# Row sums of the diagonal key tiles over GpSimd pairs, and W2 butterflies in blocks of three and five, in a two-layer adaLN kernel

## The reference, cut to what matters

```python
qkv = x @ W_qkv + b_qkv                      # 16 heads of 32
scores = jnp.einsum('bhqd,bhkd->bhqk', q, k) / np.sqrt(HEAD_DIM)
scores = jnp.where(causal, scores, NEG)      # causal, 2048 x 2048
probs = jax.nn.softmax(scores, axis=-1)
ctx = jnp.einsum('bhqk,bhkd->bhqd', probs, v)
...
hidden = fwht(silu(x @ W1.T) * (x @ W3.T))   # Walsh-Hadamard over 2048
out = hidden @ W2.T
```

## Time and profile before

| | us | share of the span |
|---|---|---|
| median of three executions | 2040.35 | |
| profiled execution | 2039.48 | |
| its span | 2037.5 | 100% |
| PE busy | 1942.6 | 95% |
| PE weight loads busy | 1392.5 | 68% |
| DVE busy | 1066.4 | 52% |
| ACT busy | 636.8 | 31% |
| POOL busy | 470.9 | 23% |

### The profile page before, as it was taken

One profiled execution on the slowest core, in us unless ns is written; L12 is line 12 of the kernel. 1 busy time (PEld: TensorE's weight loads), 2 busy tenths in 40 slices (PEclk: granted clock), 3 DMA queues, 4 the chain that ended last, 5 costly groups with the idle time before them and its releaser, 6 DMA issues. The chain is left out here.

```text
span 2037.5 us, 25525 instructions
## 1 busy us (share of the span) xinstructions
PE 1942.6 (95%) x10068; PEld 1392.5 (68%) x10068; DVE 1066.4 (52%) x1836; ACT 636.8 (31%) x1153; POOL 470.9 (23%) x409
## 2 busy tenths in 40 slices
PE   6999999999999998899999999997999889999998
PEld 4677545555555544688888888885787668888886
DVE  4456877676666633853434343435442674434334
ACT  3231345555555564332111211113221241111111
POOL 0122666667645166300000000002000510000000
PEclk9999999999999998999999999999999899999999
DMA  9654422421421103110000000002000011000002
GB/s 316 220 162 134 95 53 44 95 53 44 94 43 33 33 2 135 57 42 32 26 6 32 31 32 1 1 1 86 11 6 11 21 42 41 32 22 21 6 1 83
DMA packets 61718, 111.84 MB, mean 55 GB/s; under 512 B 6000, under 2 KB 21248, under 8 KB 61568
## 3 DMA queue, kind: packets, MB, share of 16 engines
q1 hardware_dynamic: 54144, 85.05, 14.5%
q0 software_dynamic: 7456, 25.18, 4.2%
HBM read 84.77 MB, written 25.44 MB: 54 GB/s over the span
## 5 line engine op out<-in xcount | busy, mean ns | idle before, releaser
L452 DVE TENSOR_REDUCE part_max<-banks 128x1 f32<-128x512 f32 (+2 forms) x640 | 357.2, 614 | 153.4 <-PE banks L424 93.5
L923 ACT ACTIVATE probs<-banks 128x512 f32<-128x512 f32 (+3 forms) x640 | 310.6, 539 | 279.7 <-PE banks L850 141.0
L424 PE MATMUL banks<-kst,qst 96*128 96x512 f32 (+2 forms) x640 | 261.1, 416 | 12.8 <-DVE part_max L452 9.1
L846 PE MATMUL banks<-qst,kst 98*128 98x512 f32 (+2 forms) x640 | 250.7, 412 | 0.2 <-ACT probs L923 0.2
L1448 DVE TENSOR_TENSOR tokens_a<-banks,tokens_a 128x512 f32<-128x512 f32 x224 | 151.5, 688 | 69.8 <-PE banks L216 69.0
L1473 DVE TENSOR_TENSOR tokens_b<-banks,tokens_b 128x512 f32<-128x512 f32 x64 | 44.2, 691 | 258.3 <-ACT tokens_b L1392 258.2
L214 PE MATMUL banks<-f_d_hi,f_hid_hi 128*128 128x512 f32 x432 | 170.0, 393 | 6.7 <-issue 3.6
L214 PE MATMUL banks<-h_hi,f_w_first 128*128 128x512 f32 x448 | 174.6, 390 | 0.0
L216 PE MATMUL banks<-h_hi,f_w_first 128*128 128x512 f32 x448 | 174.4, 389 | 0.0
L215 PE MATMUL banks<-h_lo,f_w_first 128*128 128x512 f32 x448 | 174.3, 389 | 0.0
L216 PE MATMUL banks<-f_d_hi,f_hid_lo 128*128 128x512 f32 x432 | 168.3, 389 | 0.0
(11 more groups left out here) (192 smaller groups left out, 3269.6 us busy)
## 6 DMA issues: line engine op xcount, KB each, us to landing
tokens_a<-in_L_wmod SPq DMA_DIRECT2D x12, 1024.0 KB, 7.0
qst<-q_hi SPq DMA_DIRECT2D x32, 256.0 KB, 6.1
kst<-k_hi SPq DMA_DIRECT2D x32, 256.0 KB, 8.3
x<-in_L_attn_x SPq DMA_DIRECT2D x4, 1024.0 KB, 13.2
q_hi<-qk_out_hi POOLq DMA_DIRECT2D x16, 256.0 KB, 3.1
q_lo<-qk_out_lo POOLq DMA_DIRECT2D x16, 256.0 KB, 3.2
k_hi<-qk_out_hi POOLq DMA_DIRECT2D x16, 256.0 KB, 4.2
k_lo<-qk_out_lo POOLq DMA_DIRECT2D x16, 256.0 KB, 4.3
```

What stands on the lines that cost most here:

```text
L424: mm = nc.tensor.matmul(dst[:, 0:wide], qst[n % QS][0:BIASROW, h, P * t:P * t + P], kst[(NB * g + c) % KS][0:BIASROW, h, 0:wide], start=Tr ...
L452: nc.vector.tensor_reduce(part_max[:, n % 2, ht, c:c + 1], max_bank(slot)[:, 0:wide], AX_X, ALU.max).then_inc(max_read, 1)
L846: mm = nc.tensor.matmul(dst[:, c0:512], kst[ck % KS][0:BIASROW + 2, h, at:at + P], qst[n % QS][0:BIASROW + 2, h, c0:512], start=True, stop ...
L923: nc.scalar.activation(probs[:, q % PS, h, c0:512], score_bank(sh)[:, c0:512], ACT.Exp, scale=SCALE).then_inc(exp_done, 1)
```

## The change

Diagonal steps become pairs too. In the first diagonal step POOL adds the two tiles over the 384 queries that both see, in the second over the 128 that both see. PE sums the pair with one set of that width, and the 128 queries that only the step's first tile sees with another set of width 128 (`narrow_sums`). Only the first step of blocks 0, 4, 8 and 12 stays as it was. The sum of a diagonal pair stands right behind the step's own context matmuls. The diagonal's pair index counts on with the others (76 pairs instead of 48), so that ACT, DVE and SP wait for them: ACT before it overwrites the tiles, DVE before it transposes bank 7, SP before it loads the projection's weights.

The butterflies of a slice are cut: three behind the first diagonal step's pair, five behind the second's. The slice's store and the next slice's load follow the eighth, and loads now alternate between two buffers.

```diff
-                return off_before(n) + i
+            pair_index = {}
+            for s, (n, i) in enumerate(steps):
+                if off_diagonal(s) or n % NB or i:
+                    pair_index[s] = len(pair_index)
+            def pair_column(s):
+                n, i = steps[s]
+                return P * max(2 * i + 1 - TB * (n % NB), 0)
...
-                sp.wait_ge(pairs_used, off_before(NQ))
+                sp.wait_ge(pairs_used, len(pair_index))
...
+                    if step % 8 == 7:
+                        pool.wait_ge(fw_step, step + 1)
+                        pool.dma_start(w2m[:, :, FW * c:FW * c + FW], fw[c % 2]).then_inc(fw_stored, 16)
+                        if c + 1 < SLICES:
+                            load_columns(c + 1)
...
-                        nc.gpsimd.tensor_tensor(pairs[o % 2][:, h, :], probs[:, 2 * s % PS, h, :],
-                                                probs[:, (2 * s + 1) % PS, h, :], ALU.add).then_inc(pair_ready, 1)
+                        nc.gpsimd.tensor_tensor(pairs[o % 2][:, h, c0:512], probs[:, 2 * s % PS, h, c0:512],
+                                                probs[:, (2 * s + 1) % PS, h, c0:512], ALU.add).then_inc(pair_ready, 1)
...
-                    if off_diagonal(s):
+                    if s in pair_index:
                         add_pair(s)
-                    elif i == 2 * (n % NB) and n in mixed_at:
-                        butterflies(mixed_at[n])
+                    if not off_diagonal(s) and n in mixed_at:
+                        for step in range(0, 3) if i == 2 * (n % NB) else range(3, 8):
+                            butterfly(8 * mixed_at[n] + step)
...
-                        if not diagonal:
+                        if paired:
+                            if diagonal and half == 0:
+                                mm = narrow_sums(s)
                             mm.then_inc(probs_read, 1)
-                    if not diagonal:
+                    if paired:
+                        if diagonal:
+                            sum_pair(s)
                         return
...
+                def narrow_sums(s):
+                    n, i = steps[s]
+                    at = first_column(n, 2 * i)
+                    for h in range(4):
+                        mm = nc.tensor.matmul(bank[7][HD * h:HD * h + HD, at:at + P], ones[:],
+                                              probs[:, 2 * s % PS, h, at:at + P], start=False, stop=False)
+                    return mm
...
-                            if q >= PS and off_diagonal(s - 2):
-                                act.wait_ge(pair_ready, 4 * off_index(s - 2) + h + 1)
+                            if s - 2 in pair_index:
+                                act.wait_ge(pair_ready, 4 * pair_index[s - 2] + h + 1)
...
                         dve.wait_ge(probs_read, quads_before(n + 1))
+                        dve.wait_ge(pairs_used, pair_index[steps.index((n, 2 * j + 1))] + 1)
```

More of the change, by code:

```diff
@@ L777, in attend_gpsimd @@
                 w2m = w2_mixed.rearrange("(c p) d -> p c d", p=P)
[L779 to L795, removed]
+                SLICES = D // FW
@@ new lines, in load_columns, with butterfly @@
+                def load_columns(c):
+                    pool.dma_start(fw[c % 2], w2[:, :, FW * c:FW * c + FW]).then_inc(fw_loaded, 16)
+                def butterfly(step):
+                    c, r, odd = step // 8, step % 8 // 2, step % 2
+                    if step % 8 == 0:
+                        pool.wait_ge(fw_loaded, 16 * (c + 1))
+                        if c:
+                            pool.wait_ge(fw_stored, 16 * c)
+                    elif odd == 0:
+                        pool.wait_ge(fw_step, step)
+                    half = 1 << r
+                    src = fw[(c + r) % 2].rearrange("p (a b h) d -> p a b (h d)", b=2, h=half)
+                    dst = fw[(c + r + 1) % 2].rearrange("p (a b h) d -> p a b (h d)", b=2, h=half)
+                    nc.gpsimd.tensor_tensor(dst[:, :, odd, :], src[:, :, 0, :], src[:, :, 1, :],
+                                            ALU.subtract if odd else ALU.add).then_inc(fw_step, 1)
+                    if step % 8 == 7:
[3 more added lines that the diff above has]
+                            load_columns(c + 1)
@@ L797, in add_pair @@
                 def add_pair(s):
-                    o = off_index(s)
+                    o, c0 = pair_index[s], pair_column(s)
                     if o >= 2:
@@ L862, in sum_pair @@
                     n, i = steps[s]
-                    o = off_index(s)
+                    o, c0 = pair_index[s], pair_column(s)
                     pe.wait_ge(pair_ready, 4 * (o + 1))
                     for h in range(4):
-                        mm = nc.tensor.matmul(bank[7][HD * h:HD * h + HD, :], ones[:], pairs[o % 2][:, h, :],
-                                              start=(i == 0), stop=False)
+                        mm = nc.tensor.matmul(bank[7][HD * h:HD * h + HD, c0:512], ones[:], pairs[o % 2][:, h, c0:512],
+                                              start=(i == 0), stop=(i == 2 * (n % NB) + 1))
                     mm.then_inc(pairs_used, 1)
@@ L879, in context @@
                         pe.wait_ge(ones_ready, 3)
+                    paired = s in pair_index
                     for half in range(2):
@@ L897, in context @@
                             mm = nc.tensor.matmul(bank[7][HD * h:HD * h + HD, c0:512], ones[:],
-                                                  probs[:, q % PS, h, c0:512], start=(kt == 0),
-                                                  stop=(last and half == 1))
+                                                  probs[:, q % PS, h, c0:512], start=(kt == 0), stop=False)
                         mm.then_inc(probs_read, 1)
+                def narrow_sums(s):
[5 more added lines that the diff above has]
+                    return mm
                 for s, (n, i) in enumerate(steps):
```

9 lines of the change are left out of this document (2 added, 7 removed).

## The result

| | before | changed |
|---|---|---|
| median of six executions, us | 2040.59 | 2031.45 |
| lowest and highest | 2036.48 to 2042.89 | 2026.07 to 2033.62 |
| ratio, 95% interval | | 0.9951 (0.9940 to 0.9962) |
| span of the profiled execution | 2037.5 | 2030.1 |

The change takes 9.1 us by the medians, 7.8 to 12.2 by the interval. The forecast was 2033.0, a gain of 7.4 against the median shown then; the sum behind it was 6.5, and that lies outside the interval.

What follows compares the result with a forecast made beforehand. PE's own work was taken as the bound (busy 95% of the span). 10.2 us of PE less waits of 0.25, 1.2, 1.2, 0.7 and 0.3 gave 6.5, from 2039.48 to 2033.0 us; range 2029 to 2039.

Steps and rivals of the forecast that it cites:

- PE's columns: Diagonal row sums on PE: 0.61 us gained in each of 12 first steps, 0.18 in 16 second, 10.2 in all.
- The subtraction that gave 0.25: Second diagonal step: 0.68 us for sets of 256 and 128, less 0.43 for 256 columns, leaves 0.25 for 128.
- the gain passes DVE: Block 9: DVE idles 3.47 and 0.41 us, longer than the 0.61 and 0.18 gained, so it starts earlier by as much.
- POOL's adds: New diagonal adds on POOL: 1.01 us at width 384, 0.45 at 128, from a line through widths 512 and 256.
- The waits: PE waiting for POOL in blocks 14, 15 and into 7, plus the last load: 3.65 us off the gain.
- Block 7: Start of block 7: its first pair comes late behind five butterflies and two DMA issues on POOL; PE waits 0.7 us.
- Second diagonals: Second diagonal steps of blocks 14 and 15: PE waits 0.6 us each for POOL's pair, 1.2 for two.
- The last load: Projection's weights and gate, issued behind the last diagonal sum: cover used up but hardly exceeded, 0.3 us, range 0 to 1.5.
- Rival 1: Narrow matmul sets bound by a 42 ns issue floor: second diagonals gain nothing, 6.2 us less 3.65, 2037 us; chance 25%.
- Rival 3: POOL's narrow adds cost a full 1.29 us at every width, so PE waits more: 2052 us, slower; chance 6%.
- Rival 4: DVE sets the pace between block ends, PE's gain becomes waiting for reductions: about 2040 us; chance 7%.
- Rival 2: Waits smaller by about 1.3 us, low-clock stretches at block starts absent for another 1.7: 2030 us; chance 12%.

Runs made afterwards that it cites:

- the step table: Two profiles each of the diagonal sums before (one with sums as before, POOL held, 2041.64 us) and changed (one run again, 2029.44), cut into steps, shorter duration kept.
- the second comparison: The changed kernel run once more, unaltered, against the kernel before, also for a second profile: 2029.44 us, ratio 0.9949.
- two kernels: Changed kernel with all eight butterflies behind the first diagonal step, 2075.84 us (32.4 of waits); changed kernel with each diagonal add done twice, 2073.70 us (26.4).

## Why the prediction was right, point by point

**PE's columns: right, a little low.** Predicted 0.61 for a first diagonal step and 0.18 for a second, 10.2 in all. Measured 0.63 to 0.65 and about 0.2, some 10.9 in all. With the waits taken off, the first steps of blocks 14 and 15 fit (0.35 + 0.27 = 0.62; -0.40 + 1.07 = 0.67); the second step of block 15 is a little short (-0.52 + 0.64 = 0.12). The subtraction that gave 0.25 for a set of 128 was 0.03 high. That the gain passes DVE, argued from the idle time in the earlier trace rows, holds: the two idles have become shorter and not vanished.

```profile
561.82 5.45 DVE L453 TENSOR_REDUCE part_max<-banks 128x1 f32<-128x512 f32 x10 [2.84 <-PE banks L425]
567.54 0.72 DVE L957 STREAM_TRANSPOSE early_gate<-banks 128x512 f32<-128x512 f32 x1 [0.28 <-PE banks L873]
```

3.47 - 0.63 = 2.84: exactly what the step before it gained.

**POOL's adds: right.** 1.01 and 0.45 predicted, 1.00 to 1.03 and 0.46 measured. The line through two widths was good at a third and a fourth.

**The waits: right in kind and in all places but one, 1.2 us too large.** Predicted 3.65, measured 2.5 by the delays of the steps in the first profile, 2.7 with the load of the second:
- Block 14 first: 0.25, measured 0.27 (742.13 + 0.64 = 742.77, started 743.04). Block 15 first: 1.2, measured 1.07. Block 7: 0.7, measured 0.50.
- Second diagonals: 0.6 each. Block 15's is 0.64. Block 14's is nothing. I took the pattern of block 15 for both, and it isn't the same: in block 14 the next block's scores stand between POOL's start and the context, in block 15 there is no next block.

```profile
744.80 1.71 POOL L810 TENSOR_TENSOR pairs_own<-probs 128x128 f32<-128x128 f32 x4 [1.81 <-ACT probs L942]
744.84 1.17 PE L853 MATMUL banks<-qst,kst 98*128 98x512 f32 x4
745.94 0.64 PE L894 MATMUL banks<-probs,tokens_a 128*32 128x256 f32 x8
746.62 0.40 PE L894 MATMUL banks<-probs,tokens_a 128*32 128x128 f32 x8
746.83 0.40 PE L873 MATMUL banks<-pairs_own,ones 128*32 128x128 f32 x8
```

These four score matmuls take 1.1 us, and POOL is done before PE asks.
- The last load: 0.3, measured 0 and 0.25. In the first profile the gate landed in 5.4 us and the weights in 5.2, and the scaling came 5.91 us behind the transpose, as before. In the second the gate took 5.8, and everything behind it came a quarter of a microsecond later. So the cover is used up, as the prediction says.

**The sum, and some luck in the time.** 10.2 - 3.65 = 6.5 predicted; 8.3 by the step table. Both terms were off the same way, the columns by 0.7 too low and the waits by 1.2 too high. The time of 2033.0 came nearer than its sum: it was named from one execution that lay 1.1 us under the median of the six. Behind the 9.1 of the medians (and 11.0 of the second comparison) stand another 1 to 3 us that lie in the clock, or in chance: the intervals hold 8.3. Whether the changed kernel has fewer stretches at the lower clock on the whole is open. The profiles don't say: in attention there are four such stretches in the changed kernel's first profile, two in its second, two in that before.

**The rivals.** Rival 1, a floor of 42 ns a matmul: refuted. Eight matmuls of width 128 start every 0.22 us, 27 ns each. The Trainium skill (TensorE: Matmul & The Clock Gate, Part 1) has some 62 ns for a matmul when hardware decoding is off, which the prediction weighed. By that figure such a set would take 0.5 us, an estimate; the row's 0.22 says that this rate doesn't bind here. Rival 3, a narrow add at full price: refuted by 0.46; doubling the adds shows how steep that side is. Rival 4, nothing moves: refuted by the ratio and by DVE's idle time. Rival 2 is half right: the measured 2031.45 lies midway between the forecast and its 2030, and the waits were smaller by 1.2 us, though not because the adds were cheaper; of the clock nothing is shown.

**What the prediction didn't see.** That POOL's store and load move with the butterflies, and that at blocks 4 and 8 they could meet the loads of keys and queries. It counted both issues as time on POOL only. In the changed kernel that cost nothing, because the pairs happen to hold POOL back until the loads that PE waits for are in; without them it costs 8 us by the medians and 11 in the profile, about as much as the change brings.

## What to carry to other kernels

Work that goes from the bound engine to a helper brings its columns back in full, less what the helper is late, and lateness has to be walked place by place: the second diagonal step had slack in block 14 and none in block 15. A helper's order is also the order of its DMAs, so ask of every moved block of work which transfers it moves beside which, and which of those the bound engine needs next. Where single stretches run at half clock in changing places, compare step by step and keep the shorter of two profiles: that told 0.2 us a step, where the comparison of whole runs couldn't tell 2 us.

## What the hardware showed that I had not expected

- Two transfers of 512 KB from POOL's queue beside keys and queries from SP's went with a landing of `qst<-q_lo` in 12.9 us instead of 9.0, and PE waited 4.75 us for `kst<-k_hi`, 0.73 before. Issued right behind such loads, at 394.0, the same store left `qst<-q_lo` at 8.3 us.
- In two kernels PE's waits cost more than their length. With 32.4 us of waits the kernel lost 44, with 26.4 it lost 42. Behind each of six waits of 3.58 to 6.90 us PE's granted clock was 0.50: 0.65 us for a set that takes 0.40. Behind two of 1.05 and 0.96 it was 1.00. In between it goes both ways: behind 1.98 us a set of 1.07 took 1.93, behind 2.22 it took 1.06.
- An add on POOL between two SBUF tiles costs 0.46, 1.01 and 1.28 us at widths 128, 384 and 512: 2.1 to 2.2 ns a column and about 0.18 us fixed, with no floor within these widths.
